# Norms with a scale: the multiplication by scale moves from GpSimd into VectorE's, the shift to ScalarE

## The reference, cut to what matters

```
x = x + latent_attention(ctx, LN(x))       # norms its inputs again, with scale and shift
x = x + moe_top1(LN(x))
x = x + context_attention(LN(x), ctx)
x = x + moe_sinkhorn(LN(x))
x = x + context_attention(LN(x), ctx)
h = LN(x);  h = h + self_attention(rms(h) * ln1_w);  x = x + h + moe_top2(rms(h) * ln2_w)
x = x + align(ctx, LN(x))
x = x + soft_slots(LN(x))
LN(v)  = (v - mean(v)) / sqrt(var(v) + eps)
rms(v) = v / sqrt(mean(v * v) + eps)
```

## Time and profile before

| | |
|---|---|
| time, median of 3 runs | 3872.72 us (3868.19 to 3879.06) |
| the profiled execution: its time | 3867.78 us |
| its span, first to last instruction | 3865.9 us |
| PE busy | 2975.2 us, 77% |
| DVE busy | 2120.6 us, 55% |
| ACT busy | 1513.0 us, 39% |
| POOL busy | 1001.7 us, 26% |
| mean granted TensorE clock | 0.873 |

### The profile page before, as it was taken

How to read it: one execution, slowest core, us unless ns; L and a number is a source line. 1 busy time by engine, 2 the same in 40 slices (tenths; PEclk the granted TensorE clock), 3 DMA queues, 4 the chain that set the end, 5 groups by cost and what they waited for, 6 DMA issues and landing times. The chain is left out here.

```text
span 3865.9 us, 43438 instructions
## 1 busy us (share of the span) xinstructions
PE 2975.2 (77%) x15086; PEld 1758.0 (45%) x15086; DVE 2120.6 (55%) x3884; ACT 1513.0 (39%) x2113; POOL 1001.7 (26%) x600
## 2 busy tenths in 40 slices
PE   4899999999994668439978599899629961049989
PEld 1545454545443542339942233333229950024457
DVE  3656555555532434338725378788327836853365
ACT  2344444444442423326523245555505630012254
POOL 1356565655572310043300100000133311001100
PEclk7899999999996788669988689999859985569999
DMA  2020000000020420045410000000025621000060
GB/s 72 5 64 7 6 6 2 4 6 6 0 66 30 150 61 1 3 151 218 174 58 1 11 4 1 6 5 2 1 106 196 217 76 17 4 22 18 37 218 22
DMA packets 87114, 198.34 MB, mean 51 GB/s; under 512 B 20387, under 2 KB 62755, under 8 KB 78880
## 3 DMA queue, kind: packets, MB, share of 16 engines
q0 software_dynamic: 18480, 108.86, 7.8%
q1 hardware_dynamic: 64608, 83.27, 7.2%
q10 hardware_dynamic: 3856, 3.95, 0.5%
HBM read 146.02 MB, written 49.76 MB: 51 GB/s over the span
## 5 line engine op out<-in xcount | busy, mean ns | idle before, releaser
L621 POOL TENSOR_TENSOR A_key_sums<-A_key_sums,A_probs 128x1024 f32<-128x1024 f32 (+1 forms) x224 | 526.9, 2371 | 228.1 <-ACT A_probs L514 228.1
L514 ACT ACTIVATE A_probs<-A_banks 128x512 f32<-128x512 f32 (+1 forms) x576 | 329.1, 597 | 384.7 <-PE A_banks L434 382.4
L564 DVE TENSOR_REDUCE A_part_max<-A_banks 128x1 f32<-128x367 f32 x768 | 354.1, 530 | 156.9 <-PE A_banks L355 155.6
L1844 DVE TENSOR_REDUCE F_part_max<-F_banks 128x1 f32<-128x512 f32 x512 | 325.3, 685 | 61.7 <-PE F_banks L1697 59.0
L1790 ACT ACTIVATE F_probs<-F_banks 128x1024 f32<-128x1024 f32 x256 | 248.3, 1023 | 240.5 <-PE F_banks L1743 240.3
L383 PE MATMUL A_banks<-A_probs,A_v_tok 128*64 128x512 f32 x1152 | 278.7, 605 | 0.0
L432 PE MATMUL A_banks<-A_q_one,A_k_one 128*128 128x512 f32 (+1 forms) x576 | 255.5, 444 | 26.2 <-ACT A_probs L514 23.1
L355 PE MATMUL A_banks<-A_k_one,A_q_one 128*128 128x368 f32 x768 | 230.3, 383 | 6.8 <-ACT A_v_tok L494 6.5
L184 POOL TENSOR_SCALAR F_r<-F_r,F_ln_w 128x512 f32<-128x512 f32 x16 | 28.8, 1812 | 783.0 <-DVE F_r L149 783.0
L434 PE MATMUL A_banks<-A_q_two,A_k_two 128*128 128x512 f32 (+1 forms) x576 | 227.1, 394 | 0.0
L355 PEld LDWEIGHTS A_banks<-A_k_one,A_q_one 128*128 128x128 f32 x768 | 147.3, 192 | 94.6 <-DVE A_part_max L564 58.5
(11 more groups left out here) (577 smaller groups left out, 6357.8 us busy)
## 6 DMA issues: line engine op xcount, KB each, us to landing
Hm_staged<-in_H_w SPq DMA_DIRECT2D x6, 1024.0 KB, 5.5
moe_in_D<-A_zeros SPq DMA_DIRECT2D x1, 6003.0 KB, 25.8
moe_in_F<-A_zeros SPq DMA_DIRECT2D x1, 6003.0 KB, 25.3
D_tile_in<-moe_in_D SPq DMA_DIRECT2D x23, 261.0 KB, 5.1
F_tile_in<-moe_in_F SPq DMA_DIRECT2D x23, 261.0 KB, 5.1
H_phi<-in_H_w SPq DMA_DIRECT2D x5, 1024.0 KB, 5.6
H_w<-in_H_w SPq DMA_DIRECT2D x5, 1024.0 KB, 4.9
D_y_tok<-moe_out_D SPq DMA_DIRECT2D x8, 512.0 KB, 5.5
```

The source lines that it names most:

```text
L514: act.activation(probs[0:kw, j, kt % RING, blk * BLK:(blk + 1) * BLK], ps[0:kw, half % 3, :], ACT.Exp, scale=1.0 / 8.0).then_inc(s["exp_re ...
L564: dve.tensor_reduce(part_max[:, i // 3, i % 3:i % 3 + 1], ps[:, MAX_BANKS[i % 3], 0:PIECE], AX.X, ALU.max).then_inc(s["piece_max"], 1)
L621: pool.tensor_tensor(key_sums[0:kw, j, :], before, probs[0:kw, j, kt % RING, :], ALU.add).then_inc(s["summed"], 1)
L1844: op = dve.tensor_reduce(part_max[:, maximum_at(hd, qt), kb:kb + 1], bank, AX.X, ALU.max)
```

## The change

In `norm_stage` the block for GpSimd is gone. Where a job has a scale, VectorE's one product of 128 x 1024 becomes two scalar_tensor_tensor of 128 x 512, one for each half: (centred x scale) x rstd. Where it also has a shift, ScalarE adds it, one Identity with a bias of 128 x 512 for each half, in the same group's list behind the four Exp, each waiting for VectorE's product of that half. VectorE's semaphore `normed` now counts halves: two for a job in every form, and ScalarE's wait on it in the Exp is counted accordingly. Stages without a scale keep their instructions.

```diff
--- before.py
+++ after.py
@@ -93,8 +93,7 @@
         ps = sc.psum()
         mean_ready, centred_ready, squared_ready = sc.sem("mean_ready"), sc.sem("centred_ready"), sc.sem("squared_ready")
         var_ready, log_ready, rstd_ready = sc.sem("var_ready"), sc.sem("log_ready"), sc.sem("rstd_ready")
-        normed, scaled = sc.sem("normed"), sc.sem("scaled")
-        affine = [n for n, job in enumerate(jobs) if job[4] is not None]
+        normed, shifted = sc.sem("normed"), sc.sem("shifted")
 
         def centred(n):
 
@@ -144,11 +143,17 @@
                                           ps[:, n % GROUP, 0:w].unsqueeze(1).broadcast_to([P, C, w]),
                                           ALU.subtract).then_inc(centred_ready, 1)
                     for n in group:
-                        _, dst, t0, w, _, _ = jobs[n]
+                        _, dst, t0, w, scale, _ = jobs[n]
                         dve.wait_ge(rstd_ready, n + 1)
-                        dve.tensor_tensor(dst[:, :, t0:t0 + w], centred(n),
-                                          rstd[:, n % GROUP, 0:w].unsqueeze(1).broadcast_to([P, C, w]),
-                                          ALU.mult).then_inc(normed, 1)
+                        if scale is None:
+                            dve.tensor_tensor(dst[:, :, t0:t0 + w], centred(n),
+                                              rstd[:, n % GROUP, 0:w].unsqueeze(1).broadcast_to([P, C, w]),
+                                              ALU.mult).then_inc(normed, C)
+                            continue
+                        for c in range(C):
+                            dve.scalar_tensor_tensor(out=dst[:, c, t0:t0 + w], in0=centred(n)[:, c], scalar=scale[:, c:c + 1],
+                                                     in1=rstd[:, n % GROUP, 0:w], op0=ALU.mult,
+                                                     op1=ALU.mult).then_inc(normed, 1)
 
             @block.scalar
             def _(act):
@@ -168,24 +173,15 @@
                         w = jobs[n][3]
                         act.wait_ge(log_ready, n + 1)
                         if n >= GROUP:
-                            act.wait_ge(normed, n - GROUP + 1)
+                            act.wait_ge(normed, C * (n - GROUP + 1))
                         act.activation(rstd[:, n % GROUP, 0:w], logvar[:, n % GROUP, 0:w], ACT.Exp,
                                        scale=-0.5).then_inc(rstd_ready, 1)
-
-            if affine:
-                @block.gpsimd
-                def _(pool):
-                    for n in affine:
-                        _, dst, t0, w, scale, shift = jobs[n]
-                        pool.wait_ge(normed, n + 1)
-                        for c in range(C):
-                            part = dst[:, c, t0:t0 + w]
-                            if shift is None:
-                                pool.tensor_scalar(part, part, scale[:, c:c + 1], None, ALU.mult).then_inc(scaled, 1)
-                            else:
-                                pool.tensor_scalar(part, part, scale[:, c:c + 1], shift[:, c:c + 1],
-                                                   ALU.mult, ALU.add).then_inc(scaled, 1)
-                    pool.wait_ge(scaled, C * len(affine))
+                    for n in group:
+                        _, dst, t0, w, _, shift = jobs[n]
+                        for c in range(C) if shift is not None else []:
+                            act.wait_ge(normed, C * n + c + 1)
+                            act.activation(dst[:, c, t0:t0 + w], dst[:, c, t0:t0 + w], ACT.Identity,
+                                           bias=shift[:, c:c + 1]).then_inc(shifted, 1)
 
 
 def norm_jobs(src, dst, scale=None, shift=None):
```

## The result

The changed kernel took 3861.12 us as the median of 7 runs (3853.41 to 3863.59), the kernel before, run beside it, 3872.72 us (7 runs, 3867.53 to 3879.06). The ratio is 0.9965, with a 95% interval of 0.9952 to 0.9978: about 13.5 us faster, between 8.5 and 18.6. The forecast was 21.4 us, and 3851 us with a range of 3844 to 3860. The sign was right; the median lies 1.1 us above the range, the 21.4 us lie outside the interval, and the gain is some six tenths of what was forecast. It is small beside the noise: the prediction called anything within 0.3% no change, and the interval, 0.22% to 0.48% faster, reaches into that. The profiled execution took 3857.31 us with a span of 3855.4 us, 10.5 us less span than before.

The account below looks back on a forecast made before the run. GpSimd's tail alone was taken to hold up the ends of nF1 and nF2, for 10.7 us each. Gains of 10.5, 10.5 and 0.4 us (nA2) made 21.4, taking 3872.7 to 3851 us; range 3844 to 3860.

Parts of the forecast that it names:

- VectorE's instructions not overlapping: In the three stages with a scale: eight half products take 6.0 us instead of 5.37; 2 us in the upper end.
- a table load: Rival, in nA2: Identity behind Exp needs ScalarE's table changed twice, 2.6 us; gain 18.8, time 3854 us; chance 0.04.
- the spread of medians: Allowance in the range for how far the median of the runs may be off: 5 us.
- VectorE's product: In the three stages with a scale: eight half products, 0.75 us each, starting 0.66 us apart, take 5.37 us.
- nF1, nF2 and the leave of the block: Both stages end with VectorE, SP issuing 0.28 us later instead of waiting for GpSimd: 10.5 us gained in each.
- TensorE's clock: Behind nF1 and nF2: TensorE's idle gap shrinks from about 24 to 14 us; nothing counted in either direction.
- the rival, which has the gain gone at 0.04 less clock: In the self-attention: a lower mean clock costs 5.6 us per 0.01; at 0.06 lost, 3885 us; chance 0.03.
- nA2: ScalarE's eight shifts delay the context's square by 1.2 us, yet SP issues at 69.8 instead of 70.25: 0.4 us gained.
- The sum: Whole kernel: gains of 10.5, 10.5 and 0.4 us add up to 21.4 us; chance of the forecast 0.81.
- nF1. GpSimd's eight go, with the wait for them: In nF1: GpSimd's eight instructions vanish, so SP issues at 2175.03 instead of 2185.57, 10.5 us gained.
- the tails are only moved: Rival: something GpSimd's tail covers ends last instead, a DMA or slow block leave; gain 0 to 21, 3862 us; chance 0.07.

Follow-up runs that it names:

- c_after: The changed kernel again, unedited: 3857.59 us against 3868.32 for the kernel before, ratio 0.9972.
- only_f: The kernel before with only nF1 and nF2 in the new form, nA2 as before: 3854.93 us against 3868.32, ratio 0.9963.
- preload: The changed kernel plus one tiny GpSimd multiply (128 x 1) in nF1: 3850.64 us against 3868.32 for the kernel before, ratio 0.9955.
- late_allred: The kernel before plus an unused GpSimd all-reduce of a 128 x 1 tile in nG, ahead of the align stage: 3872.61 us against 3868.07, ratio 1.0013.
- no_allred: The changed kernel with the second mixture of experts' all-reduce made a plain copy (different result computed): 3852.77 us against 3871.99 for the kernel before.
- pool_two: The kernel before with a second operation, plus 0.0, in GpSimd's scale multiply in nF1 and nF2: 3852.90 us against 3871.99, ratio 0.9952.
- f_preload: The kernel before with nF1 and nF2 new, nA2 old, plus the tiny GpSimd multiply in nF1: 3850.43 us against 3868.07, ratio 0.9951.

## Why the prediction was right and where it was wrong

The prediction had the local work right and the sum too large by one term that it did not have. That the time still fell within 1.1 us of the range's end is luck: the upper end had been widened for VectorE's instructions not overlapping, for a table load and for the spread of medians, and neither of the first two occurred.

*VectorE's product.* Right: 5.39 us for eight against 5.37, each 0.746 us in nF1 and nF2. With both inputs in SBUF and a scalar per partition the operation costs what L1450 costs. As in the two L1836, one starts 0.66 us after the other and some 0.08 us before it has ended. By the rule that the prediction took from "The DRAIN you can't avoid" (the Trainium skill, "VectorE: DVE Perf Modes") it would have been 6.0. The prediction left out half of that section: it also says that an instruction that isn't held starts earlier, and that is what the trace shows here.

*nF1, nF2 and the leave of the block.* Right: 10.52 and 10.50 us measured against 10.5, with SP some 0.27 us behind VectorE.

*TensorE's clock.* Right to leave it out: the router's matmuls took 13.82 us behind 13.71 us of pause as behind 24.21. The self-attention did not move by more than chance: nF-nG is 20.4 us shorter, where the two tails make 21.0. From SP's first DMA to the first square of nF2 it took 589.9 us in both profiles of the kernel before and 591.5 and 590.7 in those of the changed one, at a granted clock of 0.93 before and 0.92 after. Over all profiles it is 587.0 to 591.3 us with the old nF1 and 590.7 to 594.0 with the new one. So the rival, which has the gain gone at 0.04 less clock, did not occur; a loss of one or two us behind the shorter pause is left open.

*nA2.* Right in each part (the square 1.3 us late, predicted 1.2; shifts of 4.99 us, no table load), and 0.3 us gained from the first product on, 0.4 predicted. That is below what these timings can tell, so it is shown by the trace alone. The rival of a table load did not occur, so what one would have added in nA2, by the rows or by the Trainium skill's 2.66 us ("ScalarE: Activation LUTs", "What ACT_TABLE_LOAD costs"), was not put to the test. The switches that the norms do have are shorter than that: in the earlier trace rows the load takes 1.28 us, with 0.01 us in front of it and 0.02 behind.

*The sum.* Wrong by one missing term. The step that failed is "nF1. GpSimd's eight go, with the wait for them". GpSimd's eight also carried a reload of its code, which in the list of L184 stood as a MODIFY_POOL_CONFIG at 2155.5, 15 us ahead of the first scale, and cost nothing there; in the align stage it cost 7.25 us. The prediction took from that list the duration and left the queue's entry, so it priced the instructions that go and not what else they had done for those behind them. With the term the sum is 21.4 - 7.2 = 14.2 us, inside the interval of 8.5 to 18.6 and inside those of c_after and only_f; preload, which hides the load again, has the whole 21 inside its interval. The rival "the tails are only moved" was nearest in time (3862) and wrong in kind: nothing that the tail covered came to light, but something that had been hidden in front of it.

The Trainium skill states the thing in "GPSIMD Engine Reference", section "2.1 Instruction dispatch": the first call to freshly loaded code on GpSimd pays for a load of about 6 us that no instruction in the profile shows. This case's traces agree in kind: 5.7 us towards the all-reduce, and 6.7 to 7.25 us back to elementwise arithmetic. That such a time is paid again on the way back, and only where an all-reduce stands in front, is shown by late_allred and no_allred.

What stays open: why the timing of pool_two gave 6 us more than its stages add up to, and those of preload and f_preload 2 to 4 us less than 21; all lie near or inside their intervals. The stretch nB-nF varies by 4 us in identical kernels, and the end nH-end was 2 to 4 us shorter in some profiles without a reason that was looked for.

## What to carry to other kernels

An instruction that is taken from an engine may also be the one at which that engine prepares itself for all that follow: list the queue's entries of its line, not only its instructions, and ask which instruction is the first of its kind once it is gone, and whether anything hides the preparation there. Where an engine off the critical path has its own code to load, a one-column instruction in a stage in which it idles takes the load out of the way; here that was worth 7 us of a rewrite that had brought 14. And before work is moved off a slow engine, try the same work there in another form.

## What the runs showed of the hardware that was not expected

- Around an all-reduce over partitions GpSimd takes time to switch: 5.7 us from the queue's entry to the all-reduce (late_allred), 6.7 to 7.25 us back at the next tensor_tensor or tensor_scalar (preload, after, c_after, only_f, late_allred). A memset in between runs at once.
- GpSimd's tensor_scalar on 128 x 512 took 1.557 us with one operation and 0.692 us with a second one that adds an immediate 0.0; with scale and shift both per partition, 0.762.
- Where VectorE's products (both inputs in SBUF) and GpSimd's plain scale ran side by side, in nF1 and nF2, GpSimd's first scale took 3.53 us instead of 1.56, while VectorE's first three products kept their 1.22 us and only the last took 1.63; so four took 5.04 us instead of 4.63. In nA2, beside the scale with a shift, all four products took 1.22 us and GpSimd's first instruction 3.77. Without GpSimd, eight halves with a scalar per partition take 5.39.

```profile
L149 DVE TENSOR_TENSOR F_r<-g_y,nF_rstd x8: 1218/1222/1632, 2169.4 to 2791.6; 128x1024 f32<-128x1024 f32 x8
```
